# Where TensorE's operands lie in SBUF: the tiles of a hybrid block moved to chosen positions modulo 512 bytes

## The reference, cut to what matters

```
xn   = group_norm(x)                                   # layer 1: attention over 1024 positions
q,k,v= split(qkv_w @ xn + qkv_b)
x    = out_w @ (softmax(q k^T / 16) v) + out_b + xn

t    = tokens(x)                                       # layer 2: residual MLPs, attention
q,k,v= [(n + silu(n @ W1) @ W2) @ aW for each]         # n = layer_norm(t)
t    = t + (softmax(q k^T, axis=queries) v) @ Wout

n    = layer_norm(t)                                   # layer 3: mixture of 8 experts, top 2
p    = top_2(softmax(n @ gate_w))
t    = t + layer_norm'(n) + sum over the two experts e of p_e * (gelu(xf @ w1[e] + b1[e]) @ w2[e] + b2[e])
```

## Time and profile before

| | before |
|---|---|
| median of 3 runs | 1251.9 us (1251.01 to 1255.94) |
| the profiled execution | 1255.06 us, its span 1253.2 us |
| TensorE matmul busy | 1154.5 us (92%) |
| weight loads busy | 1075.5 us |
| VectorE busy | 822.1 us (66%) |
| ScalarE busy | 545.5 us (44%) |
| GpSimd busy | 342.7 us (27%) |

### The profile page before, as it was taken

The page is one execution under the profiler, slowest core; times in us unless marked ns, Lnnn a source line. Parts: engine busy times, 40 slices in busy tenths (PEclk is TensorE's granted clock), DMA queues, the critical chain, the costliest instruction groups (busy, mean ns, idle before and its releaser), DMA issues.

```text
span 1253.2 us, 25051 instructions
## 1 busy us (share of the span) xinstructions
PE 1154.5 (92%) x8118; PEld 1075.5 (86%) x8119; DVE 822.1 (66%) x1883; ACT 545.5 (44%) x995; POOL 342.7 (27%) x352
## 2 busy tenths in 40 slices
PE   6999999999999999999999335999999999999993
PEld 5897998988988889989888234899999999999992
DVE  4675475954667744768436777796797678856651
ACT  2533445432435334454334313674574556644431
POOL 0010002500004300025000325355455455555440
PEclk9999999999999999999999658899999999999996
DMA  5000000200001100011000133363563547533238
GB/s 164 1 4 31 1 1 1 69 34 1 1 2 35 68 1 1 1 35 35 1 1 1 62 112 106 104 198 53 170 201 52 155 90 216 147 59 54 55 46 273
DMA packets 66207, 82.70 MB, mean 66 GB/s; under 512 B 11105, under 2 KB 56545, under 8 KB 66145
## 3 DMA queue, kind: packets, MB, share of 16 engines
q1 hardware_dynamic: 52128, 63.48, 15.6%
q0 software_dynamic: 14016, 18.37, 8.2%
HBM read 60.85 MB, written 22.02 MB: 66 GB/s over the span
## 4 chain that ended last, share of the span: by engine, by line
PE 81%; DVE 8%; DMA 4%; issue 3%; SPq 1%; ACT 1%; DVEq 1%; POOL 0%; ACTq 0%; POOLq 0%
PE ps L1545 74%; PE ps L1625 2%; DMA w1r<-in_w 2%; PE ps L1587 1%; PE ps L1835 1%; PE ps L1558 1%; DMA rows<-acc_rows 1%; DVE w2s L1466 1%; DVE hs L1512 1%; DVE one_hot L1095 1%; DVE pick_hi L1103 1%; PE ps L1578 1%; PE ps L1634 1%; PE ps L1647 1%; DVE pick_lo L1098 1%
## 5 line engine op out<-in xcount | busy, mean ns | idle before, releaser
L1545 PE MATMUL ps<-xt,w1s 128*128 128x256 f32 x1746 | 257.8, 284 | 1.5 <-DVE xt L1476 1.5
L1545 PE MATMUL ps<-w2s,hs 128*128 128x256 f32 x1728 | 251.1, 280 | 2.8 <-DVE hs L1514 2.7
L1545 PEld LDWEIGHTS ps<-xt,w1s 128*128 128x128 f32 x1746 | 227.7, 190 | 2.1 <-DVE xt L1476 1.9
L1545 PEld LDWEIGHTS ps<-w2s,hs 128*128 128x128 f32 x1728 | 223.6, 188 | 4.2 <-issue 4.1
L944 ACT ACTIVATE h<-ps,b1t 128x256 f32<-128x256 f32 x288 | 137.3, 477 | 114.0 <-PE ps L1545 79.0
L704 POOL DMA_INDIRECT acc_rows<-y_w,now_s x72 | 119.8, 1665 | 166.2 <-issue 155.1
L1512 DVE CAST hs<-h 128x256 fp32r<-128x256 f32 x288 | 91.0, 316 | 71.0 <-ACT h L944 35.9
L1514 DVE TENSOR_TENSOR hs<-h,hs 128x256 fp32r<-128x256 f32 x288 | 123.0, 427 | 9.9
L1545 PE MATMUL ps<-xs,wh 128*128 128x512 f32 x384 | 123.1, 401 | 1.5 <-issue 1.5
L586 POOL TENSOR_TENSOR tl_r<-tl_eps,minus_half 128x4 f32<-128x4 f32 x16 | 16.2, 1014 | 350.8 <-DVE tl_eps L1216 350.8
L691 POOL DMA_INDIRECT xg<-xf_rows,now_g x76 | 93.2, 1226 | 47.3 <-POOL now_g L687 34.7
(11 more groups left out here) (213 smaller groups left out, 1871.5 us busy)
## 6 DMA issues: line engine op xcount, KB each, us to landing
w1r<-in_w SPq DMA_DIRECT2D x16, 1024.0 KB, 5.1
w2r<-in_w SPq DMA_DIRECT2D x16, 1024.0 KB, 8.9
b2t<-in_b SPq DMA_DIRECT2D x36, 128.0 KB, 2.9
xn<-in_x SPq DMA_DIRECT2D x4, 1024.0 KB, 4.9
acc_rows<-r_out SPq DMA_DIRECT2D x4, 1024.0 KB, 4.5
xf_rows<-xf SPq DMA_DIRECT2D x4, 1024.0 KB, 4.9
rows<-acc_rows SPq DMA_DIRECT2D x8, 512.0 KB, 7.4
out_tokens<-cols_out SPq DMA_DIRECT2D x8, 512.0 KB, 9.0
```

The lines of the kernel that those rows point to most:

```text
L1545: ins = t.matmul(out, left[l], right[r], start=first and n == 0, stop=last and n == 2, **more)
```

## The change

Only the allocations change: the order in which tiles are taken from the stack, and small tiles that nothing reads (`to_224`, `to_0`, `to_32`, `w1_to_32` and the like) that fill up to a position. No instruction is added, removed or moved: on each engine the same instructions stand in the same order with the same waits. What changes is where the operands lie. In the table, bytes modulo 512; "apart" is the stationary operand's position less the moving operand's, modulo 512.

| product (moving,stationary) | columns | count | before: moving, stationary, apart | after: moving, stationary, apart |
|---|---|---|---|---|
| xs,wh and xs,wl | 512 | 576 | 352, 192, 352 | 128, 128, 0 |
| us,wh and us,wl | 512 | 192 | 384, 192, 320 | 384, 128, 256 |
| xs,qs | 512 | 384 | 352, 352, 0 | 128, 128, 0 |
| qs,ks | 512 | 384 | 352, 352, 0 | 128, 128, 0 |
| wh,xs and wl,xs | 256 | 384 | 192, 352, 160 | 128, 128, 0 |
| wh,us and wl,us | 256 | 192 | 192, 384, 192 | 128, 384, 256 |
| vs,pr | 256 | 768 | 384, 352, 480 | 384, 352, 480 |
| vk,pr | 256 | 768 | 384, 352, 480 | 416, 352, 448 |
| xt,w1s, even steps | 256 | half of 1728 | 128, 256, 128 | 128, 352, 224 |
| xt,w1s, odd steps | 256 | half of 1728 | 128, 192, 64 | 128, 160, 32 |
| w2s,hs, even steps | 256 | half of 1728 | 256, 128, 384 | 416, 128, 224 |
| w2s,hs, odd steps | 256 | half of 1728 | 192, 128, 448 | 320, 128, 320 |

The diff, cut to the tiles that are operands and the tiles that fill up (what else moves are small tiles of VectorE and GpSimd):

```diff
         same_group = sb("same_group", [P, P])
-        minus_half = sb("minus_half", [P, 8])
-        minus_one = sb("minus_one", [P, 8])
...
         wh = bs("wh", [P, VB + 1, KC, C], F32R)
         wl = bs("wl", [P, VB + 1, KC, C], F32R)
+        xn = bs("xn", [P, KC, T])
+        xs = [bs(f"xs{i}", [P, KC, T], F32R) for i in range(2)]
+        qs = [bs(f"qs{i}", [P, KC, T], F32R) for i in range(2)]
+        ks = [bs(f"ks{i}", [P, KC, T], F32R) for i in range(2)]
+        tok = bs("tok", [P, NT, C])
+        prob = bs("prob", [P, 2, T])
+        bs("to_224", [P, 56])
+        pr = [bs(f"pr{i}", [P, 2, T], F32R) for i in range(2)]
+        bs("to_0", [P, 8])
+        xf = bs("xf", [P, NT, C])
...
+        vs = [sb(f"vs{i}", [P, NT, C], F32R, here) for i in range(2)]
+        here.close()
+        v32 = sb("v32", [P, NT, C], F32, here)
+        sb("to_32", [P, 8], F32, here)
+        vk = [sb(f"vk{i}", [P, 2, C], F32R, here) for i in range(2)]
+        here.close()
...
         q_bias = bs("q_bias", [P, KC])
...
-        xn = bs("xn", [P, KC, T])
-        xs = [bs(f"xs{i}", [P, KC, T], F32R) for i in range(2)]
-        qs = [bs(f"qs{i}", [P, KC, T], F32R) for i in range(2)]
-        ks = [bs(f"ks{i}", [P, KC, T], F32R) for i in range(2)]
-        tok = bs("tok", [P, NT, C])
-        prob = bs("prob", [P, 2, T])
-        pr = [bs(f"pr{i}", [P, 2, T], F32R) for i in range(2)]
...
+        es("to_512", [P, 16])
         xg = es("xg", [P, 2, SUB, C])
...
-        now_g = es("now_g", [P, 2, SUB], I32)
-        now_s = es("now_s", [P, 2, SUB], I32)
+        es("w1_to_32", [P, 8])
         w1s1 = [es(f"w1s1{i}", [P, KC, FF], F32R) for i in range(2)]
+        es("w2_to_192", [P, 40])
         w2s1 = [es(f"w2s1{i}", [P, FC, C], F32R) for i in range(2)]
...
+        es("w1_to_224", [P, 8])
+        w1s = ([es(f"w1s0{i}", [P, KC, FF], F32R) for i in range(2)], w1s1)
+        es("w2_to_32", [P, 16])
+        w2s = ([es(f"w2s0{i}", [P, FC, C], F32R) for i in range(2)], w2s1)
         b1t = es("b1t", [P, 2, FC])
-        b2t = es("b2t", [P, 2, C])
-        w1s = ([es(f"w1s0{i}", [P, KC, FF], F32R) for i in range(2)], w1s1)
-        w2s = ([es(f"w2s0{i}", [P, FC, C], F32R) for i in range(2)], w2s1)
+        now_g = es("now_g", [P, 2, SUB], I32)
+        now_s = es("now_s", [P, 2, SUB], I32)
```

More of the change, by code:

```diff
@@ L115, in hybrid_block_kernel @@
         wl = bs("wl", [P, VB + 1, KC, C], F32R)
+        xn = bs("xn", [P, KC, T])
[8 more added lines that the diff above has]
+        xf = bs("xf", [P, NT, C])
+        here = ExitStack()
+        tn = sb("tn", [P, NT, C], F32, here)
+        here.close()
+        xfT = sb("xfT", [P, KC, T], F32, here)
+        here.close()
+        hold_tn = bs("hold_tn", [P, NT * C])
+        here = ExitStack()
+        raw = sb("raw", [P, 14, KC * C], F32, here)
+        raw_vo = sb("raw_vo", [P, KC * C], F32, here)
+        vb_wide = sb("vb_wide", [P, KC, P], F32, here)
+        vb_col = sb("vb_col", [P, KC], F32, here)
+        here.close()
+        us = [[sb(f"us{n}{i}", [P, KC, T], F32R, here) for i in range(2)] for n in range(2)]
+        here.close()
+        x2 = sb("x2", [P, NT, C], F32, here)
+        r_out = sb("r_out", [P, NT, C], F32, here)
+        here.close()
+        hold_r1 = sb("hold_r1", [P, 8192], F32, batch_scope)
+        vs = [sb(f"vs{i}", [P, NT, C], F32R, here) for i in range(2)]
+        here.close()
+        v32 = sb("v32", [P, NT, C], F32, here)
+        sb("to_32", [P, 8], F32, here)
+        vk = [sb(f"vk{i}", [P, 2, C], F32R, here) for i in range(2)]
+        here.close()
+        hold_r2 = sb("hold_r2", [P, 4096], F32, batch_scope)
+        minus_half = bs("minus_half", [P, 8])
+        minus_one = bs("minus_one", [P, 8])
         q_bias = bs("q_bias", [P, KC])
@@ L122, in hybrid_block_kernel @@
         gate_sb = bs("gate_sb", [P, KC, E])
-        xn = bs("xn", [P, KC, T])
-        xs = [bs(f"xs{i}", [P, KC, T], F32R) for i in range(2)]
-        qs = [bs(f"qs{i}", [P, KC, T], F32R) for i in range(2)]
-        ks = [bs(f"ks{i}", [P, KC, T], F32R) for i in range(2)]
-        tok = bs("tok", [P, NT, C])
-        prob = bs("prob", [P, 2, T])
-        pr = [bs(f"pr{i}", [P, 2, T], F32R) for i in range(2)]
+        spare = bs("spare", [P, 1])
         gn_bn = bs("gn_bn", [P, KC, 2, 6])
@@ L152, in hybrid_block_kernel @@
         tl_nb = bs("tl_nb", [P, 2, NT])
[L153 to L181, removed]
         batch_scope.close()
@@ L256, in hybrid_block_kernel @@
         w2r = es("w2r", [P, 2, FC * C])
+        b2t = es("b2t", [P, 2, C])
+        es("w1_to_224", [P, 8])
+        w1s = ([es(f"w1s0{i}", [P, KC, FF], F32R) for i in range(2)], w1s1)
+        es("w2_to_32", [P, 16])
+        w2s = ([es(f"w2s0{i}", [P, FC, C], F32R) for i in range(2)], w2s1)
         b1t = es("b1t", [P, 2, FC])
-        b2t = es("b2t", [P, 2, C])
-        w1s = ([es(f"w1s0{i}", [P, KC, FF], F32R) for i in range(2)], w1s1)
-        w2s = ([es(f"w2s0{i}", [P, FC, C], F32R) for i in range(2)], w2s1)
+        now_g = es("now_g", [P, 2, SUB], I32)
+        now_s = es("now_s", [P, 2, SUB], I32)
         ex_scope.close()
```

## The result

The changed kernel takes 1249.98 us, the median of 11 runs (1245.33 to 1251.62), against 1255.58 for the kernel before over its 11 runs beside it (1250.9 to 1257.05). The ratio is 0.9963, with a 95% interval of 0.9946 to 0.998. A second measurement of both gave 0.9964 (0.9946 to 0.9982). So the change is a gain of about 4.6 us in 1255 (2.5 to 6.8 by the interval), half of the 9.6 us that were forecast. The time itself lies in the stated range, but that is partly the baseline's doing: over more runs the kernel before has a higher median than the 1251.9 us from which the forecast started.

A forecast was written before the change was run, and what follows sets the result against it. PE was taken as saturated, its pitch set by operand distance. Terms 2.4 + 0.5 + 2.6 + 1.0 - 0.4 + 2.8 + 0.7 = 9.6 us off the 1251.9 us median gave 1242; range 1228 to 1253.

The forecast's parts named there:

- The rival by which positions do nothing: All matmuls: pitches differ for reasons other than operand positions, so the time stays at 1251.9 us; chance 0.13.
- Parts 1 and 2: 512-column projections: xs,wh and xs,wl to 0 apart, 2.4 us off; us,wh and us,wl to 256, 0.5 off.
- parts 7 and 8: Experts' steps: even steps to 224 apart, 2.8 us off; odd steps to 32 and 320, 0.7 off.
- best-pitch rival: Experts' steps: all 3456 products fall to about 113.3 ns, 15.9 us off instead of 3.5, time 1230; chance 0.22.
- Part 5: 256-column projections wh,xs and wl,xs, from 160 to 0 apart: 117 ns taken, 1.0 us off.
- Part 6: 256-column projections wh,us and wl,us, from 192 to 256 apart: a loss of 0.4 us.
- Part 3: vk,pr products, from 480 to 448 apart: 116.7 to 113.3 ns, 2.6 us off.
- The steps get worse: Experts' steps: unseen distances run at 119.6 ns, costing 5.9 us instead of saving 3.5; time 1250 to 1267, chance 0.16.

The follow-up runs named there:

- sweep_pairs: Small separate kernel, long rows of identical products at 16 operand distances, 256 and 512 columns; settled pitches 117.5 to 120.0 ns and 226.7 to 234.2 ns.
- sweep_moving: Small separate kernel, rows of 48 products of 256 columns at 8 distances and 8 positions of the moving tile; 120.0 ns at 0, 116.7 at 224.
- sweep_steps: Small separate kernel running only the experts' pattern, six products and six, for 64 pairs of distances; means 116.3 to 119.7 ns over 63 pairs.
- vk_back: Changed kernel without the pad before vk, so vk is again 480 from pr; qs,ks 229.2 ns, vk,pr 116.7 ns.
- best_of_sweep: Changed kernel with experts' weights 64 above xt and hs, moving projection weights in own tiles 224 below xs and us, vs 192 from pr; ratio to before 0.9933.
- best_again: Same program as best_of_sweep, timed again beside the changed kernel: ratio to before 0.9934, median 1246.15 us against the changed kernel's 1251.06.

## Why the prediction was wrong

**What held.** PE sets the end, the pitch follows the distance between the operands, and the distance counts modulo 256: all confirmed, by the sweep and by `us,wh`, which at 256 apart has the pitch of 0. The rival by which positions do nothing is out: the sweeps have 226.7 against 233.3 ns (sweep_pairs) and 116.7 against 120.0 (sweep_moving) for the same instructions in one trace. The rule of the Trainium skill (TensorE: Matmul & The Clock Gate, "Step-by-step: what each phase is for"), that loading the next weights doesn't steal read bandwidth from the running matmul, doesn't give these numbers. That it is the two reads that get in each other's way is the prediction's reading and remains argued: no run leaves the weight loads out. Parts 1 and 2 were right in kind and a little small, -2.9 and -1.05 instead of -2.4 and -0.5: `qs,ks` had been read over its 12 products, the first six of which have not settled, while the projections stay at the settled 226.7.

**The step that failed: parts 7 and 8, the steps, 3.5 forecast and 1.2 measured.** The working gave the even steps 116.7 ns because `vk,pr` has it at the same distance modulo 256. That pitch belongs to rows of 24 equal products. In groups of six that alternate with others the same distance gives 117.5 (sweep_steps, h,b), and 64 pairs span only 116.3 to 119.7. The forecast had this objection itself, as an argument for the best-pitch rival, and did not turn it against its own price. It also took each step for one pair, where three of eight pieces mix the two buffers; so `w2s` moving with `w1s` loading was not 0 apart in every group before, as it says, but 64 or 192 in these. For the odd steps it expected little, and little came. But their own pair got worse, and what they gained came from the mixed pieces.

**Part 5**, 1.0 off forecast, 0.1 on measured: the middle between two bounds was taken for a distance that no row of 256 columns showed, and it was the worst of all with 160, 120.0 ns. Distance 0 was known to be good at 512 columns, but that says nothing for 256: the sweep has 0 as the best of the one and among the worst of the other. **Part 6** moved to the same 120.0 and cost 0.7 instead of 0.4.

**Part 3**, 2.6 forecast, 1.8 measured, and the 1.0 us of `qs,ks` behind it, which no part priced. The 113.3 ns were right for the rows behind `qs,ks`; those behind projections run at 117.8. The working said that what keeps its distance keeps its pitch. The runs showed that a run of products inherits a state: at 64 and 192 one of two pitches, and for 512 columns at 0 slower products at the start, half of the 12 before the change and all 12 behind a `vk,pr` of 113.3. vk_back shows the coupling directly.

In the profiled pair another 1.9 us or so went to waits, at the first load and in the steps that wait for weights, where the forecast had allowed for a part of a microsecond.

Two small readings of the working are off and change nothing in its sum: the clock is under 2.4 GHz in four slices around the routing and in the last one, not in three, and the pitch at which the steps would eat the gain of the other parts is 117.9 + 6.1/3.456 = 119.7 ns, not 119.5.

**The rivals.** "The steps get the best pitch" is ruled out for the placement of the change by its trace, and for every other of the 63 pairs by sweep_steps, with `hs` where `xt` is. "The steps get worse" did not happen: none of the new distances settles above 120.0 in the sweeps, and the steps gained 1.2 us. What no rival held was the plain outcome: the same mechanism at half the size.

## What to carry to other kernels

Where PE is saturated with float32r products of 256 or 512 columns, lay the stationary and the moving tile at the same position modulo 256 bytes for 512 columns, and away from 0, 128 and 160 for 256; a tile that plays both parts should be two. In this block it gave 2% of the 512-column projections and up to 2.4% of a 256-column product (1% in the steps), and 0.7% of the whole at best; the sweeps' settled pitches differ by 3% (512) and by 3 to 6% (256). Read such a price from a stretch with the same pattern of runs as the place where it is to be used: a pitch of 24 equal products doesn't hold for groups of six, a step that works ahead mixes two buffers' positions, and a product whose own operands don't move can still change its pitch.

## What the runs showed of the hardware

Two pitches that hold themselves at one distance, 113.3 and 117.8 ns at 64 and 192 bytes, chosen by what ran before, were not expected; nor that a shift by 32 bytes matters at all. Why the period is 256 bytes, and what holds a pitch, is open.

At least a part of the spread of the times has a cause of its own. best_of_sweep and best_again are one program; their profiled spans are 1247.2 and 1242.0 us. PE in the stretch after a pause near 357 us, first best_of_sweep, then best_again (time, busy and count, granted clock):

```profile
355.00:364.00 9.00, 7.02 (x35) 0.81 0.02 5
```

```profile
355.00:364.00 9.00, 7.59 (x51) 1.00 0.02 5
```

And the timeline's first row after the pause, in the same order (start, time, operation, count, idle time before it):

```profile
358.21 1.07 PE L1566 MATMUL ps<-xs,wh 128*128 128x512 f32 x2 [1.98 <-issue]
```

```profile
357.96 0.72 PE L1566 MATMUL ps<-xs,wh 128*128 128x512 f32 x2 [1.37 <-issue]
```

In the one execution the clock was 0.81 of 2.4 GHz over these 9 us and PE ran some products at 1.2 GHz; in the other it stayed at 2.4. best_of_sweep, 0.4 us ahead before the pause, is 1.7 behind by 362 us: 0.6 because its pause is longer, 1.5 because of the slower products (seven of them have 427 ns instead of some 232). Up to 704 us that stays within 0.3 us, and at 728, in the routing, it is 4.5. The granted clock from 715 to 730 us was 0.50 and 0.57, from 700 to 790 us 0.64 and 0.70. I take the clock for the cause there too, which the runs did not test. The gain of the whole change is of that size, which is why the traces, laid over each other product by product, say more here than single times do.
